# Local attention with 56-column score tiles, four value products a head moved to GpSimd, and four-channel DMAs

## What is computed

```python
x = x + _L0_conv_ref(_gn(x), ...)     # windowed attention, 7 x 7 tokens a window, 16 heads
x = x + _L1_conv_ref(_gn(x), w_out, b_out)

def _L1_conv_ref(x, w_out, b_out):    # local attention, 5 x 5 neighbours, 8 heads of 8 channels
    patches = extract_patches(x)                       # zero-padded, 25 shifts
    p = patches.reshape(N, NHEADS, hdim, K2, H, W)
    q = x.reshape(N, NHEADS, hdim, 1, H, W)
    scores = (p * q).sum(axis=2, keepdims=True)
    att = jax.nn.softmax(scores, axis=3)
    out = (p * att).sum(axis=3).reshape(N, D, H, W)
    return jnp.einsum('ndhw,od->nohw', out, w_out) + b_out[None, :, None, None]
```

## Time and profile before

| | us |
|---|---|
| median of 3 runs | 1965.46 (1964.26 to 1965.99) |
| the profiled execution | 1962.19 |
| its span, first to last instruction | 1960.4 |
| busy: PE / DVE / ACT / GpSimd | 1557.5 / 1627.2 / 1044.7 / 1162.3 |
| mean granted TensorE clock | 0.897 of full speed |

### The profile page before, as it was taken

One profiled execution on the slowest core, in us unless ns is written; L12 is line 12 of the kernel. 1 busy time (PEld: TensorE's weight loads), 2 busy tenths in 40 slices (PEclk: granted clock), 3 DMA queues, 4 the chain that ended last, 5 costly groups with the idle time before them and its releaser, 6 DMA issues.

```text
span 1960.4 us, 53519 instructions
## 1 busy us (share of the span) xinstructions
PE 1557.5 (79%) x21545; PEld 789.1 (40%) x21545; DVE 1627.2 (83%) x2105; ACT 1044.7 (53%) x1927; POOL 1162.3 (59%) x843
## 2 busy tenths in 40 slices
PE   5889999999999999244986949859598595994935
PEld 3667777777777777100221212212122121221413
DVE  5987777777777777479999999899999999999724
ACT  3566677766777666234455554554645545444200
POOL 4434544444545445004869969698796987964800
PEclk9999999999999999675997969969799697996968
DMA  6000000000000000422014140141401404005069
GB/s 266 1 1 33 4 29 33 0 33 0 33 0 33 0 41 14 115 52 52 2 45 112 29 114 16 43 113 28 111 20 43 113 25 113 21 14 223 23 231 401
DMA packets 46596, 126.42 MB, mean 64 GB/s; under 512 B 12644, under 2 KB 24932, under 8 KB 41316
## 3 DMA queue, kind: packets, MB, share of 16 engines
q1 hardware_dynamic: 46436, 124.04, 20.5%
HBM read 79.04 MB, written 38.54 MB: 60 GB/s over the span
## 4 chain that ended last, share of the span: by engine, by line
PE 51%; DVE 28%; issue 10%; ACT 5%; SPq 2%; DMA 1%; DVEq 1%; POOLq 0%; POOL 0%; ACTq 0%
PE PS L1380 11%; PE PS L1267 8%; DVE PS L1140 7%; PE PS L1357 7%; DVE arena L1159 6%; PE PS L1255 6%; PE PS L1343 5%; PE PS L1221 4%; PE PS L1246 3%; DVE consts L1101 3%; DVE arena L1148 2%; PE PS L1400 2%; DVE arena L1053 2%; DVE arena L1134 2%; PE PS L1225 2%
## 5 line engine op out<-in xcount | busy, mean ns | idle before, releaser
L777 POOL TENSOR_TENSOR arena<-arena 128x1856 f32<-128x1856 f32 (+8 forms) x182 | 670.8, 3726 | 237.5 <-ACT arena L911 188.5
L1159 DVE TENSOR_TENSOR arena<-arena,PS 128x1568 f32<-128x1568 f32 x382 | 658.9, 1781 | 26.8 <-PE PS L1380 25.2
L1343 PE MATMUL PS<-arena,consts 128*32 128x285 f32 (+10 forms) x2176 | 252.6, 540 | 197.8 <-POOL arena L777 128.0
L1380 PE MATMUL PS<-arena,consts 32*32 32x392 f32 x12800 | 385.3, 511 | 22.8 <-DVE arena L1159 22.3
L735 POOL TENSOR_TENSOR arena<-arena,consts 128x196 f32<-128x196 f32 x512 | 294.2, 609 | 161.5 <-ACT arena L825 157.0
L953 ACT ACTIVATE PS<-arena 128x392 f32<-128x392 f32 x382 | 190.9, 501 | 344.2 <-DVE arena L1159 342.3
L1267 PE MATMUL PS<-arena 128*128 128x96 f32 x2048 | 265.7, 273 | 3.1 <-ACT arena L838 1.6
L1267 PEld LDWEIGHTS PS<-arena 128*128 128x128 f32 x2048 | 249.9, 192 | 5.3 <-issue 3.5
L1357 PE MATMUL PS<-arena,consts 128*128 128x392 f32 x400 | 193.2, 578 | 52.2 <-DVE arena L1148 52.2
L742 POOL TENSOR_TENSOR arena<-arena 128x392 f32 (+1 forms) x64 | 78.6, 1228 | 255.2 <-DVE arena L1080 255.2
L1343 PEld LDWEIGHTS PS<-arena,consts 128*32 128x32 f32 x2176 | 50.3, 115 | 396.0 <-issue 182.2
(11 more groups left out here) (97 smaller groups left out, 1663.1 us busy)
## 6 DMA issues: line engine op xcount, KB each, us to landing
arena<-x_dram SPq DMA_DIRECT2D x32, 616.0 KB, 7.5
arena<-x_dram SPq DMA_DIRECT2D x240, 77.0 KB, 2.0
arena<-in_x_dram SPq DMA_DIRECT2D x8, 1568.0 KB, 14.7
x_dram<-arena SPq DMA_DIRECT2D x8, 1568.0 KB, 5.2
attn_dram<-arena SPq DMA_DIRECT2D x256, 49.0 KB, 1.9
arena<-x_dram SPq DMA_DIRECT2D x8, 1568.0 KB, 17.6
arena<-attn_dram SPq DMA_DIRECT2D x8, 1568.0 KB, 17.6
out_dram<-arena SPq DMA_DIRECT2D x8, 1568.0 KB, 24.7
```

What stands on the lines that cost most here:

```text
L777: nc.gpsimd.tensor_tensor(tile, x_part, by, ALU.mult).then_inc(pool_tile, 1)
L1159: nc.vector.tensor_tensor(by_channel(v_tiles[n % V_RING]), shifted_values(half, k), over_channels(PS[:, 2 + n % W_BANKS, 0:PIX]), ALU.mult ...
L1343: mm = nc.tensor.matmul(PS[g * GROUP:(g + 1) * GROUP, 0, 0:(hi - lo) * cols], fold, tile[:, (g * rows + lo) * cols:(g * rows + hi) * cols] ...
L1380: mm = nc.tensor.matmul(PS[dst, 4 + i, 0:PIX], ident[src, src], tile[src, c * PIX:(c + 1) * PIX], start=done == 0, stop=done == NK - 1)
```

## The change

- **Score tiles** have 56 columns for every shift; the product of (dy, dx) and the mirrored map take different parts of the same rows, the columns that lie outside the image are zeroed once a head by four small ACT copies (`clear_borders`, new). 9 x 56 = 504 fits a bank, so there are 13 units for 13 tiles, and `part_summed` is gone. The tiles are made in the reverse order, dy = 2 first and (0, 0) last.
- **Operands**: for dx = -1 the two operands of a product on GpSimd or DVE change places.
- **Values**: in heads 0 to 6 GpSimd makes four of the 50 value products, shifts 16 and 17 of half 0 amid its scores and 21 and 22 of half 1 after them; in the last head 7 and 10 (before 9 and 9), after both scalings of head 6.
- **Totals**: a planner's step is now five totals, not one; costs of other steps change with it. The reciprocal comes before the last five value products of DVE.
- **DMAs**: x1 in DRAM gets a line of its own for each channel (`LINE`), and a load for scores or a store of a half takes its four channels in one DMA: 4 where there were 16.
- **First loads**: after pair 4 is stored, groups 0 and 2 of both score slots are loaded; groups 1 and 3 follow after pair 7.
- `room(2)` shifts the last buffers by two elements.

```diff
-TILE = CH * (GR + R) * (W + R)
-HALF_PLANE = [(0, 0), (0, 1), (0, 2)] + [(dy, dx) for dy in (1, 2) for dx in range(-2, 3)]
+TILE = CH * (GR + R) * W
+HALF_PLANE = [(dy, dx) for dy in (2, 1) for dx in range(-2, 3)] + [(0, 2), (0, 1), (0, 0)]
-STORES = 16 * GROUPS * CH
+STORES = 16 * GROUPS
+LINE = R * W + BP * HW
-RECIPROCAL_AT = 47
+RECIPROCAL_AT = 5
-SHARE_AT = [9, 17]
-POOL_SHARE = [[range(0), range(0)]] * (LH - 1) + [[range(16, NK), range(16, NK)]]
+SHARE_AT = 10
+POOL_SHARE = [[(16, 17), (21, 22)]] * (LH - 1) + [[range(18, NK), range(15, NK)]]
...
-            order += own[0][:2] + [("scale", j - 2, 0), ("scale", j - 2, 1)] + own[0][2:] + own[1] + [("scale", LH - 1, 0)]
+            order += [("scale", j - 2, 0), ("scale", j - 2, 1)] + own[0] + own[1] + [("scale", LH - 1, 0)]
...
-        for k in range(NK):
-            add("pe", ("total", j, k), 0.72, [("exp", j, k // KS), ("sub", j, SUB_PARTS - 1), ("total", j, k - 1) if k else None])
+        for m in range(SUB_PARTS):
+            add("pe", ("total", j, m), 3.4, [("exp", j, m), ("sub", j, SUB_PARTS - 1), ("total", j, m - 1) if m else None])
...
+        room(2)
         lden_of_rows = room(GROUPS * PIX).rearrange("p (i n) -> p i n", i=GROUPS)
...
-            tile = ring[RING_AT[step] % S_RING][:, 0:GROUPS * rows * cols]
-            return (tile.rearrange("p (g h w) -> p g h w", g=GROUPS, h=rows),
-                    X[:, :, r0:r0 + rows, c0:c0 + cols],
-                    X[:, :, r0 + dy:r0 + dy + rows, c0 + dx:c0 + dx + cols])
+            tile = ring[RING_AT[step] % S_RING][:, 0:GROUPS * rows * W]
+            here, there = X[:, :, r0:r0 + rows, R:R + W], X[:, :, R:R + rows, R + dx:R + dx + W]
+            if dx == -1:
+                here, there = there, here
+            return tile.rearrange("p (g h w) -> p g h w", g=GROUPS, h=rows), here, there
...
-                for c in range(CH):
-                    off = ((g // 2 * C + j * HD + a * CH + c) * BP + BP // 2 * (g % 2)) * HW + r0 * PIX
-                    at = x1_flat[0:1, off:off + 1]
-                    src = bass.AP(at.tensor, at.offset, [[PIX, r1 - r0], [1, RAW]])
-                    sp.dma_start(raw[RAW_SLOT[n]][c * GROUP + r0:c * GROUP + r1, g * RAW:(g + 1) * RAW],
-                                 src).then_inc(raw_loaded[RAW_SLOT[n]], 16)
+                off = (g // 2 * C + j * HD + a * CH) * LINE + BP // 2 * (g % 2) * HW
+                at = x1_flat[0:1, off:off + 1]
+                src = bass.AP(at.tensor, at.offset, [[LINE, CH], [PIX, GROUP], [1, RAW]])
+                sp.dma_start(raw[RAW_SLOT[n]][:, g * RAW:(g + 1) * RAW], src).then_inc(raw_loaded[RAW_SLOT[n]], 16)
...
-                    for c in range(CH):
-                        dst = attn_dram[b2, j * HD + half * CH + c].rearrange("bp rg n -> (bp rg) n")
-                        sp.dma_start(dst[first:first + GROUP], o_loc[half][c * GROUP:(c + 1) * GROUP, i]).then_inc(o_stored[half], 16)
+                    dst = attn_dram[b2, j * HD + half * CH:j * HD + half * CH + CH].rearrange("c bp rg n -> c (bp rg) n")
+                    sp.dma_start(dst[:, first:first + GROUP], o_loc[half][:, i]).then_inc(o_stored[half], 16)
...
-            for bp in range(BP - 1):
+            for bp in range(BP // 2 + 1):
                 store_x1(bp)
...
+            for n in range(2):
+                for g in range(0, GROUPS, 2):
+                    load_for_scores(n, g)
+            for bp in range(BP // 2 + 1, BP):
+                store_x1(bp)
+            sp.wait_ge(x1_stored[1], 16 * (BP // 2 - 1))
+            for n in range(2):
+                for g in range(1, GROUPS, 2):
+                    load_for_scores(n, g)
...
+                by = shifted_values(half, k), over_channels(sc[j % 2][:, k, :])
+                if ALL_SHIFTS[k][1] == -1:
+                    by = by[::-1]
...
+            def clear_borders(j):
+                for dx in (-2, -1, 1, 2):
+                    slots = sorted(slot_of(-dy, -dx) for dy, x in HALF_PLANE if x == dx)
+                    n, width = len(slots), abs(dx)
+                    first = 0 if dx > 0 else W - width
+                    maps = sc[j % 2][:, slots[0]:slots[-1] + 1:KS].rearrange("p n (h w) -> p n h w", w=W)
+                    nc.scalar.activation(maps[:, :, :, first:first + width],
+                                         no_rows[:, 0:n * GR * width].rearrange("p (n h w) -> p n h w", n=n, h=GR), ACT.Copy)
```

More of the change, by code:

```diff
@@ L136, in pool_order @@
             order.append(("score", j, t, a))
-            for half in range(2):
-                if n >= SHARE_AT[half] and (n - SHARE_AT[half]) % 2 == 0:
-                    order += own[half][:1]
-                    own[half] = own[half][1:]
-        assert not own[0] and not own[1]
+            if n >= SHARE_AT and (n - SHARE_AT) % 2 == 0:
+                order += own[0][:1]
+                own[0] = own[0][1:]
+        order += own[1]
+        assert not own[0]
     return order
@@ L210, in merge_orders @@
             add("act", ("exp", j, m), 1.85, [("sub", j, m)])
-        add("dve", ("reciprocal", j), TIMES["reciprocal"], [("total", j, NK - 1)])
+        add("dve", ("reciprocal", j), TIMES["reciprocal"], [("total", j, SUB_PARTS - 1)])
         for half in range(2):
@@ L222, in merge_orders @@
+        for t in range(S_TILES):
             rows, cols = shape_of(t)
[L223 to L225 removed]
+            before = ("copy", j, t - 1) if t else ("copy", j - 1, S_TILES - 1) if j else None
             for a in range(2):
[L227 to L235 removed]
@@ L236, in merge_orders @@
-            ends = ("sum", ("score", j, t, 1)) if last else ("part", ("score", j, t, 1))
-            copies = 1 if t == 0 else 2
-            add("act", ("copy", j, u), copies * (0.2 + 0.83e-3 * min(PIX, (hi - lo) * W)),
-                [ends] + ([("weight", n) for n, v in enumerate(V_ORDER) if v[1] == j - 2][-1:] if j >= 2 else [])
-                + ([("total", j - 2, NK - 1)] if j >= 2 else [("pixels", "v", 0, 1, GROUPS + 1)])
-                + ([s for s in RING_ORDER if s[:2] == ("value", j - 2)][-1:] if j >= 2 else []), 0.6 if j else 0.1)
+                n = RING_AT[("score", j, t, a)]
@@ L242, in merge_orders @@
+                add("pe", ("sum", ("score", j, t, a)), 0.2 + 1.67e-3 * rows * cols,
+                    [("score", j, t, a), before, ("sum", RING_ORDER[n - 1]) if n else None], 0.6 if j else 0.1)
+            add("act", ("copy", j, t), (1 if HALF_PLANE[t] == (0, 0) else 2) * 0.5,
+                [("sum", ("score", j, t, 1)), ("borders", j)], 0.4 if j else 0.1)
     for j in range(LH):
@@ L266, in merge_orders @@
     orders = {eng: [] for eng in todo}
-    rank = {"weight": 0, "exp": 1, "evict": 1, "sum": 0, "part": 1, "copy": 2, "total": 3, "pixels": 4}
+    rank = {"weight": 0, "exp": 1, "evict": 1, "sum": 0, "copy": 2, "total": 3, "borders": 3, "pixels": 4}
     while any(todo.values()):
@@ L1389, in _ @@
                 else:
[L1390 to L1391 removed]
+                    sum_scores(step[1])
             for bp in range(BP):
```

168 lines of the change are left out of this document (61 added, 107 removed).

## The result

The changed kernel takes 1974.38 us (median of 6 runs, 1971.5 to 1981.22), the kernel before 1963.85 (6 runs, three of them shown ahead of the prediction). The ratio is 1.0059, 95% interval 1.0041 to 1.0078: slower by 8 to 15 us. The forecast was 1970 with 1950 to 1984, a small loss the likeliest sign: it put the loss at 4.3 us, and between the two medians it is 10.5. The profiled executions differ by 12.4 us (1974.55 against 1962.19), their spans by 12.2 (1972.6 against 1960.4).

A forecast was written before the change was run, and what follows sets the result against it. PE was taken to bound the first half of a local head, DVE the second. Terms -1.4 - 2.7 + 5.6 + 2.8 = +4.3 us on the median 1965.46 gave 1970, range 1950 to 1984.

The forecast's parts named there:

- Score tiles: Each local head: 34 sums with up to 2 copies each become 26, the wait before the maximum ends; gain 3.2 us.
- Four value products, swapped operands: Heads 0 to 6: DVE rid of 6.8 us a head; on GpSimd 2.95 us each, dx = -1 tiles 1.90 ns a column.
- Totals in lumps: Steady heads: five runs of totals on PE stall DVE 14 us; period 123.8 against 122.98, +5.6 us over seven.
- GpSimd's loop: Steady heads: 109.8 us of work, 5.7 after DVE's end and 3.6 make 119.1 plus ring waits, below 123.
- Head 0's scores: First local head, scores on DVE: 57.7 us become 55, of which products 51.3 and slow-clocked PE some 2; -2.7 us.
- Entry loads: Loads after the last store of x1, on four DMA engines: landed at 829 instead of 830.4; -1.4 us, range -7.4 to +4.
- Last stores: End of the local stage: 8 issues on 4 engines, 67 ns a row, 19.1 us against 16.3; +2.8, range -8.0 to +11.
- A: Rival at entry and last stores: DMAs spread over 16 engines, -7.4 and -8.0, 1953 us; chance 0.12.
- B: Rival in steady heads: totals do not hold DVE, GpSimd's loop sets a pace of 120; -21, 1943 us; chance 0.10.
- C: Rival on GpSimd: swap does nothing or makes other layouts dear, +2 us a head, 1984 us; chance 0.13.

The follow-up runs named there:

- the kernel with the spread stores: Changed kernel with each store of a half as 16 DMAs of 32 rows, one a channel, where the change has 4: 1972.17 us, ratio 1.0041.
- paced and with the new order of pixels: Changed kernel, one DMA a channel, fives only in last head; elsewhere total k behind value sum 1.6 k, half 0's score pixels normalised first: 1953.74 us.
- the kernel with the spread loads: Changed kernel with each load for scores as 16 DMAs, one a channel of 32 rows, where the change has 4: 1962.95 us, ratio 0.9993.
- spread totals: Changed kernel, one DMA a channel, fives only in last head; elsewhere single total k behind value sum of DVE's product 1.6 k: 1936.92 us.

## Why the prediction was right, step by step

- **Score tiles.** Right in effect: the wait before the maximum is gone (22.5 us to 1.5), also with single totals (1.5). But the lumps by themselves bring it down to 3.3 in the kernel before, so the new tiles are not its only cure.
- **Four value products, swapped operands.** Right: 3.00 us each where 2.95 was forecast, and GpSimd's timeline has shift (1,-1) at 3.43 where the order of operands before gave 4.16:

```profile
1087.56 3.01 POOL L767 TENSOR_TENSOR arena<-arena 128x1568 f32<-128x1568 f32 x1 [0.92 <-PE PS L1325]
...
1095.48 3.43 POOL L756 TENSOR_TENSOR arena<-arena 128x1792 f32<-128x1792 f32 x1 [1.59 <-PE PS L1325]
```

  That is 1.91 ns a column (3.43 / 1792). Without the swap the same tile of 1792 columns takes 4.11 us, 2.29 ns a column (head 2 of that kernel, start 1217.79), so the operands' places make the difference.
- **Totals in lumps.** Right in mechanism and size: PE full from the subtractions to its first idle time at 1231.05, 48.7 us ("some 44"), busy for 39.89 of the head's last 49.38 us, 81% ("85 to 90%"), 12.4 us of waits a head ("a stall of 14"), values ending 94.1 to 95.6 us after the subtractions ("95.1"), a period of 123.63 ("123.8"). One sum was out: the first run took 4.9 us (granted clock 0.71 on average), not 5.5, and value 15 was summed after 41.4 us, not 43.4. The walk also looked at the wrong product: the last that waits is DVE's 14th, released by value 10 behind the fifth run, 35.3 us after the subtractions where 13 x 1.70 = 22.1 would do. The stall of 13 us is there all the same, and it is what the walk was for. Single totals in the changed kernel confirm the cause.
- **GpSimd's loop.** Right where it could be seen: in head 3 its first score product starts at 1281.91, 5.5 us after DVE is through with head 2's values and begins its next maximum (1276.38); the forecast has 5.7.
- **Head 0's scores.** The size was off, -4.8 for -2.7. The products took 51.35 us (51.3 forecast); the 2 us for PE at its low clock did not come, though the granted clock was 0.50 from 882 to 887 us and 0.82 on average over these scores.
- **Entry loads: the term that was most wrong.** "Landed at 829 where it was 830.4" should have been 835.7 (838.87 less the 3.2 of the windowed stage). The four engines were right: from 829 to 835 us the share is 0.26, four of 16 (the 0.17 above is the mean with the end of the loads in it). The price of a row was not. I gave most rows 0.11 to 0.15 us, but while the value loads ran beside them on all engines (a share of 0.84, 158 GB/s) a row of 2464 B took 16 x 0.84 x 2464 B / 158 GB/s = 0.21 us, more than my upper bound of 0.185, and alone on four engines (0.26, 81 GB/s) still 0.13. Over 192 rows that is 0.167 a row from the issue to the end (32.1 / 192) where the forecast has 0.132, and the range's +4 lay under the +5.3 measured.
- **Last stores.** The mechanism was right, the size was 4.1 for 2.8. A row takes 16 x 0.27 x 1568 B / 92 GB/s = 74 ns, where I took 67, and 256 rows make 18.9 of the 20.4 us; that the rest is SP's first issues is an estimate. With an outer count of 4 the share is 0.27, four engines of 16; with 32 it was 0.40, and 0.40 again in the kernel with the spread stores (1891.1 to 1899.1 us).
- **Rivals.** A (spread over 16 engines) fell with the share of 0.27. B (no hold by totals) fell with the 87.0 us of waits, but its pace of 120 is what five of the kernels without lumps then ran at (119.5 to 120.5); the sixth with the four products on GpSimd, paced and with the new order of pixels, has 122.3. C was priced right, +2 a head, and did not happen.

The forecast of 1970 lies 4.4 us under the measured median, nearer than its parts deserve. The two DMA terms were 6.7 and 1.3 us too small; head 0's scores and the periods, 2.1 and 1.1 us too large, took some of that back, and the first three executions of the kernel before, from which the forecast starts, have a median 1.6 us above that of all six. The mechanisms of the heads and of the last stores were foreseen; that the errors left the time well inside the range is in part luck.

## What to carry to other kernels

Cost an edit's order and not only its work: a total takes PE 0.85 us alone and 0.70 in a run of five (3.49 / 5), yet the runs cost 9.4 us a head in the kernel before, because PE was full there already (55.00 of 55 us) and a ring of three tiles lets DVE run only three products ahead. Where one engine is full for half a period, anything that it can do later belongs later, but ahead of whoever waits for the last of it. Before you merge four DMAs into one, read from the DMA share what the new outer count gets: with a count of 4 it was 0.26 to 0.27 in the loads and stores here, where the loads of 32 rows, with the value loads, ran at 0.92 to 1.06 (816 to 826 us of the kernel with the spread loads). Merging cost nothing amid the stage (periods of 123.54 and 123.38 with the spread loads and stores, 123.63 without) and 10.8 and 4.4 us at its ends in the profiled executions.

## What the runs showed that was not expected

- The distance of an engine's end to its neighbour's is not slack. GpSimd ended 4 us before DVE, and 3.9 us more of work still cost 2.2 a head, because PE takes one of its tiles before the totals that DVE's products wait behind.
- A kernel with fewer waits can have several limits close together: with spread totals the period stayed between 119.5 and 120.5 us when the reciprocal's wait was taken away, when GpSimd started earlier and when PE was spared some work. Each step moved it by 0.7 us or less. Two of them together made it worse, 122.3.
- PE stood still for 2.1 us at the end of a reload at 429 GB/s, and the granted clock was lower behind it (0.66 over 5 us, then 1.00 again), in one of two kernels with the same work there. Its cause is open.
- The windowed stage, with the same work in all of these kernels, ended at times up to 6.4 us apart (last store of x1 at 798.0 to 804.4) from one profiled execution to the next.
